# Two tiles a turn in the vector engine's loop of a group-norm and displaced-blur kernel

## The reference

```
x = x + displace(gn(x), offset)

gn:        g = v.reshape(B, 32, C // 32, H, W)
           (g - mean(g)) / sqrt(var(g) + 1e-5)
displace:  off_px  = offset * 64;  off_int = round(off_px);  sub = off_px - off_int
           shifted = x moved by off_int pixels, zero where it leaves the image
           kern    = exp(-(kx*kx + ky*ky) / 0.5), 3 x 3, normalised, kx and ky moved by sub
           out     = depthwise 3 x 3 convolution of shifted with kern
```

## Time and profile before

| what | value |
|---|---|
| median of three runs | 979.16 us |
| the profiled execution's own time | 979.77 us |
| its span | 977.8 us |
| bytes read and written in HBM | 201.38 + 201.33 MB |
| DMA, mean over the span | 412 GB/s |
| VectorE busy | 828.4 us (85%) |
| TensorE busy | 787.0 us (80%), granted clock 0.889 |
| ScalarE busy | 663.7 us (68%) |
| GpSimd busy | 394.7 us (40%) |

### The profile page before, as it was taken

How to read it: one execution, slowest core, us unless ns; L and a number is a source line. 1 busy time by engine, 2 the same in 40 slices (tenths; PEclk the granted TensorE clock), 3 DMA queues, 4 the chain that set the end, 5 groups by cost and what they waited for, 6 DMA issues and landing times.

```text
span 977.8 us, 9199 instructions
## 1 busy us (share of the span) xinstructions
PE 787.0 (80%) x2132; PEld 385.9 (39%) x2132; DVE 828.4 (85%) x550; ACT 663.7 (68%) x557; POOL 394.7 (40%) x348
## 2 busy tenths in 40 slices
PE   0998988879879797897979869788687997979810
PEld 0444443434434343343434434344343443434310
DVE  7487889877698997978889999898998969798695
ACT  7778887664766747777666856678585786864661
POOL 0204156350433624014245393454935338261423
PEclk9998998989979799897989978989898898989955
DMA  8999999999999999999999999999999999999948
GB/s 365 427 401 380 428 418 430 431 431 428 429 432 410 430 431 405 431 432 430 428 409 425 397 432 390 408 429 397 433 409 430 430 432 429 431 430 429 427 184 344
DMA packets 27822, 403.10 MB, mean 412 GB/s; under 512 B 3216, under 2 KB 3216, under 8 KB 3216
## 3 DMA queue, kind: packets, MB, share of 16 engines
q1 hardware_dynamic: 27792, 402.71, 98.0%
HBM read 201.38 MB, written 201.33 MB: 412 GB/s over the span
## 4 chain that ended last, share of the span: by engine, by line
DVE 27%; DMA 24%; PE 22%; ACT 9%; POOL 8%; issue 5%; DVEq 2%; ACTq 2%; SPq 0%; POOLq 0%
PE sum_ps L287 20%; DMA xs<-x_dram 12%; DMA out_dram<-xs 12%; ACT frame L413 6%; DVE smooth L697 6%; DVE xs L701 6%; DVE xs L704 6%; DVE smooth L692 5%; DVE xs L707 4%; POOL small L251 3%; POOL small L255 2%; POOL small L258 2%; ACT unused L478 1%; POOL small L264 1%; DVEq L696 1%
## 5 line engine op out<-in xcount | busy, mean ns | idle before, releaser
L287 PE MATMUL sum_ps<-xs,bands 128*128 128x512 f32 x976 | 484.1, 654 | 37.7 <-DMA xs<-x_dram 37.5
L478 ACT ACTIVATE unused<-xs,small 128x4096 bf16 (+1 forms) x94 | 348.7, 3709 | 16.7 <-ACT small L468 7.1
L413 ACT ACTIVATE frame<-xs,small (+1 forms) x96 | 223.4, 2327 | 177.9 <-DVE smooth L697 176.1
L287 PEld LDWEIGHTS sum_ps<-xs,bands 128*128 128x128 f32 x976 | 201.3, 211 | 281.1 <-issue 271.3
L251 POOL TENSOR_TENSOR small<-small 128x3 f32<-128x3 f32 x32 | 41.5, 1296 | 545.9 <-ACT small L486 545.9
L287 PE MATMUL sum_ps<-xs,halves 128*128 128x512 f32 x496 | 228.7, 616 | 19.3 <-DMA xs<-x_dram 19.3
L692 DVE SCALAR_TENSOR_TENSOR smooth<-frame,xs 128x612 f32 (+5 forms) x96 | 163.6, 1704 | 75.2 <-ACT frame L423 61.6
L701 DVE SCALAR_TENSOR_TENSOR xs<-smooth,small,xs 128x612 f32 (+5 forms) x96 | 163.6, 1704 | 45.0 <-POOL small L264 42.7
L697 DVE SCALAR_TENSOR_TENSOR smooth<-frame,xs,smooth 128x612 f32<-128x612 f32 (+5 forms) x96 | 163.5, 1703 | 7.3 <-DVE smooth L692 3.6
L704 DVE SCALAR_TENSOR_TENSOR xs<-smooth,small,xs 128x594 f32 (+9 forms) x96 | 159.8, 1664 | 3.4
L707 DVE SCALAR_TENSOR_TENSOR xs<-smooth,small,xs 128x594 f32 (+9 forms) x96 | 159.7, 1664 | 3.4
(11 more groups left out here) (132 smaller groups left out, 275.0 us busy)
## 6 DMA issues: line engine op xcount, KB each, us to landing
xs<-x_dram SPq DMA_DIRECT2D x96, 2048.0 KB, 14.8
out_dram<-xs SPq DMA_DIRECT2D x96, 2048.0 KB, 16.9
smooth<-offset_dram SPq DMA_DIRECT2D x1, 48.0 KB, 4.2
```

Of the source, the lines that this page charges most:

```text
L287: last = nc.tensor.matmul(sum_ps[:, :], (FIRST, SAME, SECOND)[i], slot_px(n, c * BANK, (c + 1) * BANK), start=(i == 0 and c == 0), stop=(i ...
L413: nc.scalar.activation(frame[:, bass.ds(b, rows * PITCH)].rearrange("p (r c) -> p r c", c=PITCH)[:, :, LEFT:LEFT + W], xs[:, bass.ds(a, ro ...
L478: nc.scalar.activation(unused[:, :], xs[:, bass.ds(n % SLOTS * PIX, PIX)], ACT.Square, bias=neg_mean[:, i:i + 1], accum_out=squares[:, i:i ...
```

## The change

VectorE's loop runs 48 times in place of 96, and its body handles two tiles, one after the other. The register that counts the turns becomes a pair's number; the tile's number is computed from it. The code of `tile_of`, with its 16 variants, stands in the body twice.

```diff
             dve.reg_load(next_tile, words[0:1, 0:WORDS])
             dve.addr_align(256, max_nops=0)
-            with dve.Fori(0, TILES) as n:
-                tile_of(n)
+            with dve.Fori(0, TILES // 2) as pair:
+                for i in range(2):
+                    tile_of(dve.snap(2 * pair + i))
```

## The result

The changed kernel takes 1384.75 us, the median of four runs (1383.71 to 1386.98), beside 980.72 us for four runs of the kernel before. The ratio is 1.4145, with a 95% interval of 1.4116 to 1.4173. The prediction had 1087 us in a range of 1000 to 1340 us: the direction is right, the time lies outside the range, and the way it went is rival 1 and not the forecast. The profiled execution has a span of 1381.6 us, 403.8 us more than before.

What follows compares the result with a forecast made beforehand. The prediction took DMA to bound the kernel, VectorE second. It added 148 us for code fetches, less 36 us given back and 5 us for fewer branches: 979.8 + 148 - 36 - 5 = 1087 us, range 1000 to 1340 us.

Steps and rivals of the forecast that it cites:

- rival 1: VectorE's loop: all four code blocks refetched each turn, five fetches a turn, 1323 us; chance 0.24.
- Code is fetched in blocks of 128, and the next is asked for on entering one: VectorE's instruction fetch: 128 instructions a block, next one requested on entry; body goes from two blocks to four.
- Four blocks are held, and the branch back finds the head gone: VectorE's code store: holds four blocks; the fifth, behind the loop, displaces the first, so 47 back branches wait.
- What goes is only the first block: VectorE's loop: first block and the one behind it change places, two packets a turn, about 107 on q14.
- the milder case: The forecast itself: only the head is refetched at each of 47 back branches, 1087 us; chance 0.57.
- The number of stops: VectorE's fetch waits under rival 1: 47 behind back branches plus 12 + 47 = 59 further ones.
- 4.0 us a fetch: Wait for the head's code behind VectorE's back branch: 4.0 us, from 3.5 to 4.4 us.
- Emptier DMA engines make fetches cheap: Within rival 1: on an emptier queue a fetch falls to 2.5 us or less, giving 1200 to 1250 us.
- 36 us come back: VectorE's other waits partly hidden by the fetch stops: 21 us for GpSimd plus 15 us for ScalarE's frame.
- 5 us from fewer back branches: VectorE's sequencer: 48 back branches removed, 0.4 us each, showing in 23 of 96 gaps, about 5 us saved.
- DMA bound before: DMA engines in the kernel before: busy nearly throughout, 403.10 MB at 432 GB/s taking 933 of 979.8 us.

Runs made afterwards that it cites:

- pad4m: Kernel before (one tile a turn) plus 146 never-executed instructions behind the variants, body 390, the last six in a fourth block; 1419.95 us, ratio 1.4496.
- pad3off: pad3 with the loop head at slot 64 of a block in place of 0, so its 372 instructions touch four blocks; 1764.5 us, ratio 1.8068.
- pad4h: Kernel before (one tile a turn) plus 240 never-executed instructions ahead of the variants, body 484 in four blocks; 2192.95 us, ratio 2.2455.
- pad3: Kernel before (one tile a turn) plus 128 never-executed instructions behind the variants, body 372 in three blocks; 980.88 us, ratio 1.0019.
- hint2: Changed kernel plus one instruction, a prefetch hint for the back branch at the body's head; all but some 4 of the 404 us gone.
- lean2: Changed kernel (two tiles a turn) with only the ten variants each copy needs, body 303 instructions in three blocks; 980.39 us, ratio 1.0009 to the kernel before.
- pad4h_hint: pad4h plus a prefetch hint at the body's head that names the back branch; 993.03 us, ratio 1.0128 to the kernel before.

## Why the prediction was wrong

- **Code is fetched in blocks of 128, and the next is asked for on entering one.** Right. Packet counts worked out from it came true: 213 for 214 (pad4m), 352 for 354 (pad3off), 490 for 490 (pad4h), and 250 for the 250 of rival 1.
- **Four blocks are held, and the branch back finds the head gone.** Right: pad3 and hint2 show that four fit, pad4m that a fifth does not.
- **What goes is only the first block.** This is the step that failed. I took the block behind the loop to have its place where the first block stood, so that the two would alternate, two packets a turn. The runs show five a turn, rival 1. No row of before told the two apart, as the prediction said of rival 1, and yet I gave the milder case more than twice the chance. A replacement by age makes a loop one block too long lose all its blocks, not one.
- **The number of stops.** Rival 1 counted 47 + 59; there were 47 + 63 over 0.9 us.
- **4.0 us a fetch.** Mis-sized, and in both directions. Behind the back branch it was 269 / 47 = 5.7 us in the mean, elsewhere 227 / 63 = 3.6 us. The 3.1 to 4.0 us of the earlier trace rows were the time to the packet on loaded DMA engines; the changed kernel's 32 long gaps have 3.0 to 5.3 us to their first packet. What I added for the rest was 0.4 us, the packet alone. But the sequencer goes on only some 1.2 to 1.7 us after the end of its packet, with load or without: of the 2.74 us at 563 us 1.0 us is before the packet, 0.4 us the packet and 1.4 us behind it. That is why rival 1's 1323 us and the end of the range, 1340 us, fell short of 1385: with 5.7 and 3.6 us in its place the same sum gives 979.8 + 47 x (1.6 + 5.7 - 2.44) + 227 - 36 - 5 = 1394 us.
- **Emptier DMA engines make fetches cheap** (the end of rival 1, 2.5 us or less). Half right. The mean rate fell to 293 GB/s, but transfers come in bursts, and 34 of 47 back branches fell into one. The stop goes with how long L707 takes: the store of the tile just finished begins as it ends (591.74 us for an L707 that ends at 591.71). Behind an L707 of 1.4 us or less 29 of 31 stops took over 6 us. Behind one of 2.4 us or more the fetch had its packet before the store began, and all 12 took 3.5 us or less.
- **36 us come back.** Near in size, but not by its two parts. The wait for GpSimd was to give back 21 us and gave 33 (42.7 to 9.4 us). GpSimd also needed less time for the same work, 209 us busy in place of 395 (L264: 545 ns a piece in place of 1266); why was not tested. The frame wait went from 61.6 to 10.3 us, but inside a longer gap, so what it gave back can't be read off.
- **5 us from fewer back branches.** Not seen in the time: lean2 has 1.0009 (0.9993 to 1.0025). L692's wait for L707 fell there by 5.8 us, the size that was forecast, but lean2's choice trees are smaller too.
- **DMA bound before.** Right as a limit for gains, and no protection against a loss of this size: VectorE's idle time was only 134 us, and stops of 269 + 227 = 496 us made the kernel 404 us longer.

## What to carry to other kernels

A loop on VectorE's sequencer has to be counted in fetch blocks, not in instructions: blocks touched from head to end, with the offset of the head, and one for the block behind. Up to four in all cost nothing here (pad3, lean2); at five every block touched was fetched again every turn, and 18 dead instructions or a moved head were enough (pad4m, pad3off). The number of packets on the "instruction" queue tells it at once, and a hint for the back branch removed it both times it was tried, at the price of slower branches. The hint was not tried on a loop of three blocks; there is no refetch there that it could save. Fewer turns alone brought this kernel nothing. Other engines' loops were not tried.

## What was not expected of the hardware

- The refetch of one block of 8 KB takes 2.7 us at the least, though its packet is then on a DMA engine for only 0.3 to 0.6 us; behind a burst of the kernel's own transfers it takes up to 8.6 us.
- The prefetch hint keeps a four-block loop resident also where its blocks are visited with jumps (pad4h_hint, 14 packets in place of 490), and doubles the duration of VectorE's compare-and-branch of line 183 (50 to 103 ns in hint2, to 99 ns in pad4h_hint).
- Whether the block that goes is the one fetched first or the one unused for longest stays open: in all these loops both give the same packets.
